# Folding the dimension sums by accumulating transfers, and splitting step 15 of layer 1, in a recommendation tower's interaction layers

## The chip, the core and the metric

The kernel runs on one core of a Trainium2 chip. The metric is the device time of one execution in microseconds. Three executions of the kernel before gave a median of 1453.37 us (1452.75 to 1454.29).

## What is computed

For 2048 samples, 39 embedding rows of 16 numbers each are gathered from 39 tables. Two interaction layers follow, each over the 16 dimensions separately: layer 0 multiplies all pairs of the 39 fields and maps the 39x39 products to 128 values; layer 1 multiplies the 39 fields with the first 64 of these and maps 39x64 products to 128 values. ReLU results are summed over the 16 dimensions, and a small dense tower ends the work.

```python
z0 = jnp.einsum('bid,bjd->bdij', x0, x0).reshape(B, D, F0 * F0)
cur0 = relu(jnp.einsum('bdk,kl->bld', z0, W0))
next_h, direct0 = jnp.split(cur0, 2, axis=1)
z1 = jnp.einsum('bid,bjd->bdij', x0, next_h).reshape(B, D, F0 * Fk)
cur1 = relu(jnp.einsum('bdk,kl->bld', z1, W1))
return jnp.sum(jnp.concatenate([direct0, cur1], axis=1), axis=-1)
```

## The kernel before

The samples go in 16 tiles of 128, and each tile in two units of 8 dimensions (32 units, columns 8 x 128 = 1024). A unit has 6 or 7 steps of layer 0 and 20 steps of layer 1. In each step VectorE (DVE) makes a product tile z of 128x1024 (`make`, L951), and TensorE (PE) multiplies it with weights into PSUM: psA for layer 0, psB for layer 1. The steps of layer 0 of unit u+1 are strewn between the steps of layer 1 of unit u, after the steps listed in `AFTER`.

A step is whole or split. A whole step is one float32 product (`product`, L545). A split step is three float32r products (`split_product`, L575, L578, L582): ScalarE (ACT) rounds z_split to z_hi (`high`, L818), and DVE makes z_lo = z_split - z_hi (`low`, L960), which `low_before` puts on DVE right behind the make of the next step. Layer 0 splits its steps 1 and 4, layer 1 the steps in `SPLIT1`.

Each engine runs its instructions in the order of the code. ACT's `body(u)` issues the `high` of every split step of that body and then, behind all of them, `relu0(u + 1)`: 13 activations that read psA, namely two for h_pair (L763), eight for h_quad (L771), two for h_half (L796) and one for r0 (L802). The `high` of split step 1 of layer 0 of unit u+2 comes behind these on ACT, early in body u+1. `relu1(u - 1)` (L809) is issued at step 6 of body u.

The sums over the dimensions: `relu0` and `relu1` leave the ReLU results in r0 and r1 (128x2048), and DVE reduces each to 128x128 (`sum0`, L1011, every fourth body; `sum1`, L1016, every second body), both at step 18 of a body. `sum1(k)` stands in body 2k+2, `sum0(q)` in body 4q+3; the last of each stands behind the loop.

GpSimd (POOL) issues one indirect gather for each tile and field (L522), 23 for tile 0, 31 for tile 1 and 39 for each later tile, 600 in all. It waits for `x_turned` before tile t, which PE raises when it transposes the tile before the last. SyncE (SP) issues the loads of x_lay, bases, x_more and x_last.

Of the kernel before, what the change touches and what calls it, by code (L numbers as in the profile page):

```python
# [5 lines left out]
P = 128  # L6
B = 2048
F = 39
D = 16
L = 128  # L10
H = L // 2
TILES = B // P
HALVES = 2
UNITS = TILES * HALVES
DH = D // HALVES
C = DH * P
BANK = 512
# [19 lines left out]
LAYS = 1 + FQ  # L37
SPLIT0 = (1, 4)
HALF1 = 12
SPLIT1 = (2, 3, 7, 8, 9, 13, 14)  # L40
WHOLE0 = tuple(s for s in range(STEPS0) if s not in SPLIT0)
REST0 = 3
EARLY = (2, 3)
WHOLE1 = tuple(s for s in range(STEPS1) if s not in SPLIT1 or s in EARLY)
ORDER0 = SPLIT0 + WHOLE0
AFTER = (0, 1, 3, 5, 7, 9, 11)
AHEAD = 2
FIRST_AFTER = (-1, -1, 0, 1, 3, 5, 7)
NZ = 7
NS = 3  # L50
NX = 6
M1, M2 = 512, 256
# [16 lines left out]
ALU = mybir.AluOpType  # L69
ACT = mybir.ActivationFunctionType  # L70
AX = mybir.AxisListType
# [39 lines left out]
def gathers(t):  # L111

    return F - (HOT_F * HOT_GROUPS[t] if t < HOT_TILES else 0)
# [8 lines left out]
def lay_part(s):  # L122

    return divmod(s - (s > HALF1) + 1, 2) if s else (0, 0)


def hot_no(t, q):
# [9 lines left out]
def at1(u, s):  # L137

    return FIRST1[u] + s + sum(a < s for a in after(u))
# [15 lines left out]
def split1(u):  # L155

    return tuple(s for s in SPLIT1 if u > 0 or s not in EARLY)

# [17 lines left out]
def tower(nc, ids, tables, hot_ids, hot_tables, hot_consts, ident_in, dense_t, w0_a, w0_b, w1_whole, w1_split, top, top_small, y):  # L176
    ctx = ExitStack()
    with ctx:
        def sb(name, shape, dt=FP):
            return ctx.enter_context(nc.sbuf_tensor(name, shape, dt))  # L180
# [3 lines left out]
        def sb_loop(name, shape):  # L184
            return loop.enter_context(nc.sbuf_tensor(name, shape, FP))

        def sem(name):
            return ctx.enter_context(nc.semaphore(name))
# [16 lines left out]
        h_half = sb("h_half", [P, BANK])  # L205
        z_hi = [sb(f"z_hi{n}", [P, C], FR) for n in range(NS)]
        z_lo = [sb(f"z_lo{n}", [P, C], FR) for n in range(NS)]
        r0 = sb("r0", [P, 2 * C])
        r1 = sb("r1", [P, 2 * C])
# [3 lines left out]
        w1 = sb("w1", [P, len(WHOLE1), L])  # L213
        w1_hi = sb("w1_hi", [P, len(SPLIT1), L], FR)
        w1_lo = sb("w1_lo", [P, len(SPLIT1), L], FR)
        small = sb("small", [P, K1 + K2 + K2])
        feat_d = sb("feat_d", [P, B // 2])
        feat_side = sb("feat_side", [P, B], FR)
        feat_c = sb("feat_c", [P, B])
# [5 lines left out]
        h_quad = [[sb_loop(f"h_quad{n}_{k}", [P, C]) for k in range(2)] for n in range(2)]  # L225
        z = [sb_loop(f"z{n}", [P, C]) for n in range(NZ)]
        z_split = [sb_loop(f"z_split{n}", [P, C]) for n in range(NS)]
        loop.close()
# [10 lines left out]
        def half(t, u):  # L239
            return t[:, (u % 2) * C:(u % 2 + 1) * C]  # L240
# [18 lines left out]
        more_spread = [t.rearrange("p (d r) -> p d r", d=DH) for t in (feat_c[:, 0:C], feat_c[:, C:2 * C], feat_d[:, 0:C])]  # L259
        left_spread = [r1[:, c * C:c * C + DH * GROUP].rearrange("p (d r) -> p d r", d=DH) for c in range(2)]  # L260

        r0_by_b, r1_by_b = [t[:, :].rearrange("p (b d) -> p b d", d=D) for t in (r0, r1)]

        def lay(u, m):
            n = (LAYS * u + m) % NX
# [3 lines left out]
        w0_raw_b = r0[:, C:C + STEPS0 * L].rearrange("p (s l) -> p s l", s=STEPS0)  # L269
        w1_raw = r1[:, 0:len(SPLIT1) * L].rearrange("p (s l) -> p s l", s=len(SPLIT1))  # L270

# [13 lines left out]
        psB = ctx.enter_context(nc.psum_tensor("psB", [P, 2 * C], FP))  # L285
# [55 lines left out]
        z_lo_made = sem("z_lo_made")  # L341
        relu0_done = sem("relu0_done")
        relu1_done = sem("relu1_done")
        sum0_done = sem("sum0_done")
        sum1_done = sem("sum1_done")
        top_hi_made = sem("top_hi_made")
# [163 lines left out]

        @block.gpsimd
        def _(pool):
            pool.wait_ge(ids_loaded, 16)
            for t in range(TILES):
                if t >= 2:
                    pool.wait_ge(x_turned, t - 1)
                if t == 2:
                    pool.wait_ge(part_spread, 7)
                if t == 1:
                    pool.wait_ge(ids_rest_loaded, 16)  # L520
                for f in range(F - gathers(t), F):
                    nc.gpsimd.indirect_dma_start(emb[t % 2][:, f * D:(f + 1) * D], None, tables[f],  # L522
                                                 bass.IndirectOffsetOnAxis(ids_all[:, t, f:f + 1], 0)).then_inc(gathered[t % 2], 16)


        @block.tensor
        def _(pe):
# [12 lines left out]
            def product(ps, place, k, w, first, last):  # L540

                pe.wait_ge(z_made, place + 1)
                for c in range(C // BANK):
                    cs = slice(c * BANK, (c + 1) * BANK)
                    mm = nc.tensor.matmul(ps[:, cs], w[0:k, :], z[WHOLE_NO[place] % NZ][0:k, cs], start=first, stop=last)  # L545
                mm.then_inc(z_used, 1)

            def half_product(ps, place, w, last):

                pe.wait_ge(z_made, place + 1)  # L550
                for n in range(2):
                    rows = slice(n * HROWS, (n + 1) * HROWS)
                    mm = nc.tensor.matmul(ps[:, n * BANK:(n + 1) * BANK], w[rows, :],  # L553
                                          z[WHOLE_NO[place] % NZ][rows, 0:BANK], start=False, stop=last)
                mm.then_inc(z_used, 1)

            def left_product(u):
# [5 lines left out]
                for k, (v, c) in enumerate(left_groups(u)):  # L563
                    rows = slice(k * GROUP, k * GROUP + LEFT)
                    mm = nc.tensor.matmul(half(psA, v)[:, c * BANK:(c + 1) * BANK], w0[rows, ORDER0.index(STEPS0 - 1), :],  # L565
                                          z[WHOLE_NO[place] % NZ][rows, 0:BANK], start=v > u, stop=v == u)
                mm.then_inc(z_used, 1)

            def split_product(ps, place, k, w_hi, w_lo, first, last):

                n = SPLIT_NO[place]
                pe.wait_ge(z_hi_made, n + 1)
                for c in range(C // BANK):
                    cs = slice(c * BANK, (c + 1) * BANK)
                    nc.tensor.matmul(ps[:, cs], w_hi[0:k, :], z_hi[n % NS][0:k, cs], start=first, stop=False)  # L575
                for c in range(C // BANK):
                    cs = slice(c * BANK, (c + 1) * BANK)
                    nc.tensor.matmul(ps[:, cs], w_lo[0:k, :], z_hi[n % NS][0:k, cs], start=False, stop=False)  # L578
                pe.wait_ge(z_lo_made, n + 1)
                for c in range(C // BANK):  # L580
                    cs = slice(c * BANK, (c + 1) * BANK)
                    mm = nc.tensor.matmul(ps[:, cs], w_hi[0:k, :], z_lo[n % NS][0:k, cs], start=False, stop=last)  # L582
                mm.then_inc(z_used, 1)
# [14 lines left out]
            def step1(u, s):  # L598
# [4 lines left out]
                elif s in split1(u):  # L603
                    n = SPLIT1.index(s)
                    split_product(half(psB, u), at1(u, s), P, w1_hi[:, n, :], w1_lo[:, n, :], s == 0, s == STEPS1 - 1)
# [136 lines left out]
        def _(act):  # L742
# [48 lines left out]
            def relu0_rest(u):  # L791
                h = half(psA, u)
                if u >= 1:
                    act.wait_ge(z_made, at1(u - 1, HALF1) + 1)
                for n in range(2):
                    op = nc.scalar.activation(h_half[n * H:(n + 1) * H, :], h[0:H, n * BANK:(n + 1) * BANK], ACT.Relu)  # L796
                op.then_inc(h_half_made, 1)
                if u >= 4:
                    act.wait_ge(sum0_done, u // 4)
                rows = slice(0, H) if u % 4 >= 2 else slice(H, P)  # L800
                by_d = h.rearrange("p (d b) -> p b d", b=P)[H:P]
                nc.scalar.activation(r0_by_b[rows, :, u % 2 * DH:(u % 2 + 1) * DH], by_d, ACT.Relu).then_inc(relu0_done, 1)  # L802

            def relu1(u):
                act.wait_ge(z_used, at1(u, STEPS1 - 1) + 1)
                if u >= 2:
                    act.wait_ge(sum1_done, u // 2)
                by_d = half(psB, u).rearrange("p (d b) -> p b d", b=P)
                nc.scalar.activation(r1_by_b[:, :, u % 2 * DH:(u % 2 + 1) * DH], by_d, ACT.Relu).then_inc(relu1_done, 1)  # L809

            def high(place):

# [103 lines left out]

            feat_high(0)
            relu1(UNITS - 1)
            feat_high(1)
            top1_keep(0)  # L920
# [17 lines left out]
        def _(dve):  # L938
            def make(place, a, b):
# [6 lines left out]
                else:  # L946
                    n = WHOLE_NO[place]
                    if n >= NZ:
                        dve.wait_ge(z_used, WHOLE_AT[n - NZ] + 1)
                    out = z[n % NZ]  # L950
# [56 lines left out]
                    low(place - 1)  # L1007

            def sum0(q):
                dve.wait_ge(relu0_done, 4 * q + 4)  # L1010
                nc.vector.tensor_reduce(feat_d[:, q * P:(q + 1) * P], r0_by_b, AX.X, ALU.add).then_inc(sum0_done, 1)  # L1011

            def sum1(t):
                dve.wait_ge(relu1_done, 2 * t + 2)
                col = t % 2 * (B // 2) + t // 2 * P
                nc.vector.tensor_reduce(feat_c[:, col:col + P], r1_by_b, AX.X, ALU.add).then_inc(sum1_done, 1)  # L1016

            def split_top():
                dve.wait_ge(top_loaded, 32)
# [196 lines left out]
            feat_low(0)  # L1216
            split_top2()
            sum0(UNITS // 4 - 1)
            sum1(TILES - 1)
            feat_low(1)  # L1220
            hid1_low(0)
# [97 lines left out]
```

## Time and profile before

| | |
|---|---|
| median of 3 runs | 1453.37 us |
| the profiled execution's own time | 1453.96 us |
| its span, first to last instruction | 1452.2 us |
| mean granted TensorE clock | 0.991 of full speed |
| PE busy | 1417.0 us (98%) |
| DVE busy | 1381.2 us (95%) |
| POOL busy | 991.2 us (68%) |
| ACT busy | 784.1 us (54%) |

Busy shares are means over a prologue, 32 unit bodies and a tail. A busy PE is a PE with a product in flight, not one at its peak. A timeline gives starts from the begin of the span; where instructions overlap a little, the distance of two starts is what one of them costs its engine.

### The profile page before, as it was taken

What the parts mean: (1) busy time and instruction counts of PE and PEld (TensorE: products, weight loads), DVE (VectorE), ACT (ScalarE), POOL (GpSimd) and SP (SyncE); (2) the same over time, 40 slices, a digit from 0 to 9 for tenths busy, and PEclk for the clock granted to TensorE, in tenths of its full rate; (3) what the DMA queues carried; (4) which work ended last, traced back from release to release, by engine and by line L of the source; (5) the groups of instructions that cost most, each with busy time, mean ns of one, the idle gap of its engine ahead of it and who ended that gap; (6) DMA issues with size and microseconds to landing.
All of it is one profiled execution on the core that took longest, in us unless ns stands there. A gap on an engine that the chain in (4) does not pass through costs nothing.

```text
span 1452.2 us, 14669 instructions
## 1 busy us (share of the span) xinstructions
PE 1417.0 (98%) x4408; PEld 784.4 (54%) x4408; DVE 1381.2 (95%) x1243; ACT 784.1 (54%) x833; POOL 991.2 (68%) x604
## 2 busy tenths in 40 slices
PE   4899999999999999999999999999999999999999
PEld 3454555555555555555555555555555555555556
DVE  6699999999999999999999999999999999999983
ACT  1454565555455656545465555545556554565655
POOL 7788888888888888888888888888888830000000
PEclk7899999999999999999999999999999999999999
DMA  5879989998888988888898998889898887788600
GB/s 156 177 188 220 223 195 215 203 216 211 201 213 196 214 210 209 212 197 221 199 204 214 210 214 201 208 201 216 200 220 200 203 222 192 204 198 209 178 16 0
DMA packets 130779, 282.64 MB, mean 195 GB/s; under 512 B 36532, under 2 KB 61764, under 8 KB 130572
## 3 DMA queue, kind: packets, MB, share of 16 engines
q1 hardware_dynamic: 96588, 268.31, 75.3%
q0 software_dynamic: 19200, 4.95, 4.0%
q10 hardware_dynamic: 14912, 8.46, 2.0%
q8 instruction: 34, 0.56, 0.2%
q14 instruction: 45, 0.37, 0.1%
HBM read 273.67 MB, written 7.87 MB: 194 GB/s over the span
## 4 chain that ended last, share of the span: by engine, by line
PE 88%; DVE 6%; issue 2%; DMA 2%; POOL 1%; ACT 0%; SPq 0%; DVEq 0%
PE psB L545 42%; PE psA L545 14%; PE psB L575 7%; PE psB L582 6%; PE psB L578 6%; PE psB L553 2%; DVE z L951 2%; PE psA L575 2%; PE psA L578 2%; PE psA L582 2%; POOL emb L522 1%; DVE z_lo L960 1%; DVE z_split L951 1%; PE psA L565 1%; DMA bases<-x_tiles 1%
## 5 line engine op out<-in xcount | busy, mean ns | idle before, releaser
L522 POOL DMA_INDIRECT emb<-in_tbl,ids_all x600 | 991.0, 1652 | 185.0 <-issue 182.6
L545 PE MATMUL psB<-z,w 128*128 128x512 f32 x1544 | 689.1, 592 | 2.1 <-DVE z L951 2.1
L818 ACT ACTIVATE z_hi<-z_split 128x1024 fp32r<-128x1024 f32 x285 | 301.2, 1060 | 508.7 <-DVE z_split L951 446.9
L545 PEld LDWEIGHTS psB<-z,w 128*128 128x128 f32 x1544 | 292.8, 190 | 358.3 <-issue 333.6
L951 DVE TENSOR_TENSOR z<-h_quad,x_lay 128x1024 f32<-128x1024 f32 x354 | 419.4, 1215 | 0.2
L960 DVE TENSOR_TENSOR z_lo<-z_split,z_hi 128x1024 fp32r<-128x1024 f32 x285 | 349.4, 1226 | 14.4 <-ACT z_hi L818 14.4
L951 DVE TENSOR_TENSOR z_split<-h_quad,x_lay 128x1024 f32<-128x1024 f32 x222 | 266.8, 1214 | 3.0 <-DMA x_lay<-x_tiles 3.0
L771 ACT ACTIVATE h_quad<-psA 32x1024 f32<-32x1024 f32 x248 | 251.8, 1015 | 6.6 <-DVE feat_side L1036 2.9
L545 PE MATMUL psA<-z,w 128*128 128x512 f32 x516 | 243.9, 596 | 5.6 <-DVE z L951 5.6
L575 PE MATMUL psB<-z_hi,w_hi 128*128 128x512 f32 x444 | 155.9, 432 | 0.0
L545 PEld LDWEIGHTS psA<-z,w 128*128 128x128 f32 x516 | 98.1, 191 | 105.5 <-issue 92.9
L582 PE MATMUL psB<-z_lo,w_hi 128*128 128x512 f32 x444 | 138.1, 392 | 3.5 <-DVE z_lo L960 3.5
L578 PE MATMUL psB<-z_hi,w_lo 128*128 128x512 f32 x444 | 137.9, 392 | 0.0
L951 DVE TENSOR_TENSOR z<-bases,x_more 128x1024 f32<-128x1024 f32 x96 | 116.6, 1214 | 0.0
L575 PEld LDWEIGHTS psB<-z_hi,w_hi 128*128 128x128 f32 x444 | 79.8, 188 | 52.1 <-issue 38.8
L582 PEld LDWEIGHTS psB<-z_lo,w_hi 128*128 128x128 f32 x444 | 82.4, 188 | 24.8 <-DVE z_lo L960 7.2
L578 PEld LDWEIGHTS psB<-z_hi,w_lo 128*128 128x128 f32 x444 | 83.3, 188 | 18.5
L763 ACT ACTIVATE h_pair<-psA 64x1024 f32<-64x1024 f32 x62 | 62.9, 1014 | 5.7 <-PE psA L565 5.3
L809 ACT ACTIVATE r<-psB 128x1024 f32<-128x1024 f32 x32 | 33.0, 1033 | 45.0 <-PE psB L582 25.2
L575 PE MATMUL psA<-z_hi,w_hi 128*128 128x512 f32 x126 | 52.3, 496 | 0.0
L951 DVE TENSOR_TENSOR z<-bases,x_ring 128x1024 f32<-128x1024 f32 x33 | 40.1, 1214 | 10.2 <-DMA bases<-x_tiles 10.2
L951 DVE TENSOR_TENSOR z_split<-bases,x_ring 128x1024 f32<-128x1024 f32 x31 | 37.7, 1217 | 1.8 <-ACT bases L852 1.1
(122 smaller groups left out, 757.0 us busy)
## 6 DMA issues: line engine op xcount, KB each, us to landing
x_lay<-x_tiles SPq DMA_DIRECT2D x1152, 128.0 KB
x_more<-x_tiles SPq DMA_DIRECT2D x62, 468.0 KB
bases<-x_tiles SPq DMA_DIRECT2D x62, 468.0 KB
x_lay<-x_tiles SPq DMA_DIRECT2D x64, 256.0 KB
x_ring<-x_tiles SPq DMA_DIRECT2D x31, 468.0 KB
emb<-in_tbl,ids_all POOLq DMA_INDIRECT x600
x_last<-x_tiles SPq DMA_DIRECT2D x64, 128.0 KB, 10.3
x_tiles<-x_side ACTq DMA_DIRECT2D x14, 256.0 KB
```

The costliest lines, as they stand in the source:

```text
L522: nc.gpsimd.indirect_dma_start(emb[t % 2][:, f * D:(f + 1) * D], None, tables[f], bass.IndirectOffsetOnAxis(ids_all[:, t, f:f + 1], 0)).th ...
L545: mm = nc.tensor.matmul(ps[:, cs], w[0:k, :], z[WHOLE_NO[place] % NZ][0:k, cs], start=first, stop=last)
L553: mm = nc.tensor.matmul(ps[:, n * BANK:(n + 1) * BANK], w[rows, :], z[WHOLE_NO[place] % NZ][rows, 0:BANK], start=False, stop=last)
L575: nc.tensor.matmul(ps[:, cs], w_hi[0:k, :], z_hi[n % NS][0:k, cs], start=first, stop=False)
L578: nc.tensor.matmul(ps[:, cs], w_lo[0:k, :], z_hi[n % NS][0:k, cs], start=False, stop=False)
L582: mm = nc.tensor.matmul(ps[:, cs], w_hi[0:k, :], z_lo[n % NS][0:k, cs], start=False, stop=last)
L763: op = nc.scalar.activation(h_pair[n * H:(n + 1) * H, :], h[0:H, :], ACT.Relu)
L771: op = nc.scalar.activation(h_quad[u % 2][k][n * QUAD:(n + 1) * QUAD, :], h[k * QUAD:(k + 1) * QUAD, :], ACT.Relu)
L809: nc.scalar.activation(r1_by_b[:, :, u % 2 * DH:(u % 2 + 1) * DH], by_d, ACT.Relu).then_inc(relu1_done, 1)
L818: nc.scalar.activation(z_hi[n % NS][0:k, 0:cols], z_split[n % NS][0:k, 0:cols], ACT.Copy).then_inc(z_hi_made, 1)
L951: nc.vector.tensor_tensor(out[0:k, 0:cols], a[0:k, 0:cols], b[0:k, 0:cols], ALU.mult).then_inc(z_made, 1)
L960: nc.vector.tensor_tensor(z_lo[n % NS][0:k, 0:cols], z_split[n % NS][0:k, 0:cols], z_hi[n % NS][0:k, 0:cols].bitcast(FP), ALU.subtract).th ...
```

## The change

The ReLU results are written in another order (two blocks of four dimensions inside each half of r0 and r1). For all but the last sums, POOL issues two accumulating transfers inside SBUF: the first adds the second half of r0 or r1 (128x1024) onto the first, the next adds 128x512 onto 128x512. DVE then reduces 128x512 to 128x128 in place of 128x2048, and waits for the second transfer (`folded0`, `folded1`). The last sum of each kind stays one reduction, over two axes.

The transfers stand at written places in POOL's list of gathers: the first of `fold1(k)` ahead of the gather of field f of tile t with (t, f) from `FOLDS1`, else (k+4, 8); the second three gathers later; `fold0(q)` in the same way. Ahead of the first POOL waits for the ReLU results, ahead of the second for the first. The folds of the last tiles stand behind all gathers.

Besides, step 15 of layer 1 joins `SPLIT1`: 32 whole steps become split ones.

```diff
-SPLIT1 = (2, 3, 7, 8, 9, 13, 14)
+SPLIT1 = (2, 3, 7, 8, 9, 13, 14, 15)
+FD = 4
+FOLDS1 = {0: (3, 4), 1: (4, 14), 2: (5, 24), 3: (6, 35)}
+FOLDS0 = {0: (3, 20), 1: (6, 4)}
+FOLD_GAP = 3
+def fold1_place(k):
+    return FOLDS1.get(k, (k + 4, 8))
+def fold0_place(q):
+    return FOLDS0.get(q, (2 * q + 4, 25))
...
+            def fold1(k, part):
+                if part == 0:
+                    pool.wait_ge(relu1_done, 2 * k + 2)
+                    nc.gpsimd.dma_start(r1[:, 0:C], r1[:, C:2 * C], accum_op=ALU.add).then_inc(folded1, 16)
+                else:
+                    pool.wait_ge(folded1, 32 * k + 16)
+                    nc.gpsimd.dma_start(r1[:, 0:BANK], r1[:, BANK:C], accum_op=ALU.add).then_inc(folded1, 16)
...
                 for f in range(F - gathers(t), F):
+                    fold_at(t, f)
                     nc.gpsimd.indirect_dma_start(emb[t % 2][:, f * D:(f + 1) * D], None, tables[f],
...
+            fold1(12, 0)
+            fold1(12, 1)
+            fold0(6, 0)
+            fold0(6, 1)
+            for k in (13, 14):
+                fold1(k, 0)
+                fold1(k, 1)
...
-                nc.scalar.activation(r1_by_b[:, :, u % 2 * DH:(u % 2 + 1) * DH], by_d, ACT.Relu).then_inc(relu1_done, 1)
+                nc.scalar.activation(relu_out(r1, slice(0, P), u), relu_in(half(psB, u), slice(0, P)), ACT.Relu).then_inc(relu1_done, 1)
...
             def sum1(t):
                 dve.wait_ge(relu1_done, 2 * t + 2)
                 col = t % 2 * (B // 2) + t // 2 * P
-                nc.vector.tensor_reduce(feat_c[:, col:col + P], r1_by_b, AX.X, ALU.add).then_inc(sum1_done, 1)
+                out = feat_c[:, col:col + P]
+                if t < TILES - 1:
+                    dve.wait_ge(folded1, 32 * (t + 1))
+                    nc.vector.tensor_reduce(out, folded(r1), AX.X, ALU.add).then_inc(sum1_done, 1)
+                else:
+                    nc.vector.tensor_reduce(out, unfolded(r1), AX.XY, ALU.add).then_inc(sum1_done, 1)
```

## Rows read from the trace of the kernel before

**Rows 1.** The page, part 1: busy time and share of each engine.
```profile
PE 1417.0 (98%) x4408; PEld 784.4 (54%) x4408; DVE 1381.2 (95%) x1243; ACT 784.1 (54%) x833; POOL 991.2 (68%) x604
```
**Rows 2.** By window: length; busy PE, PEld, DVE, ACT, POOL; clock, DMA, GB/s.
```profile
650.00:700.00 50.00, 50.00 (x148) 26.71 (x147) 48.40 (x42) 31.23 (x34) 42.69 (x25) 1.00 0.93 218
```
**Rows 3.** DVE's waits from 150 to 1380 us: total us, times, longest.
```profile
DVE z_lo L960 <- ACT z_hi L818: 12.5, 15, 1.4
```
**Rows 4.** Timeline of PE: start, us, what; split steps, then whole ones.
```profile
707.36 0.62 PE L575 MATMUL psB<-z_hi,w_hi 128*128 128x512 f32 x2
...
708.72 1.88 PE L545 MATMUL psA<-z,w 128*128 128x512 f32 x4
710.44 3.60 PE L545 MATMUL psB<-z,w 128*128 128x512 f32 x8
```
**Rows 5.** Timeline of DVE: step 15, then the next body's first z_lo.
```profile
602.92 1.25 DVE L951 TENSOR_TENSOR z<-h_quad,x_lay 128x1024 f32<-128x1024 f32 x1
...
617.70 1.26 DVE L960 TENSOR_TENSOR z_lo<-z_split,z_hi 128x1024 fp32r<-128x1024 f32 x1
...
645.28 1.21 DVE L951 TENSOR_TENSOR z<-h_quad,x_lay 128x1024 f32<-128x1024 f32 x1
646.42 1.21 DVE L960 TENSOR_TENSOR z_lo<-z_split,z_hi 128x1024 fp32r<-128x1024 f32 x1
...
658.98 1.26 DVE L960 TENSOR_TENSOR z_lo<-z_split,z_hi 128x1024 fp32r<-128x1024 f32 x1 [1.13 <-ACT z_hi L818]
```
**Rows 6.** Timeline of ACT: the block `relu0`, then the next z_hi.
```profile
645.44 2.06 ACT L763 ACTIVATE h_pair<-psA 64x1024 f32<-64x1024 f32 x2 [0.22 <-PE psA L565]
...
656.98 1.02 ACT L802 ACTIVATE r<-psA 64x1024 f32<-64x1024 f32 x1
657.91 1.99 ACT L818 ACTIVATE z_hi<-z_split 128x1024 fp32r<-128x1024 f32 x2
```
**Rows 7.** Timeline of DVE: a sum of layer 1 and the instruction behind it.
```profile
608.63 2.27 DVE L1016 TENSOR_REDUCE feat_c<-r 128x128 f32<-128x2048 f32 x1
610.83 1.21 DVE L951 TENSOR_TENSOR z<-h_quad,x_lay 128x1024 f32<-128x1024 f32 x1
```
**Rows 8.** Groups by line: busy us, mean ns; products of 512 columns.
```profile
L951 DVE TENSOR_TENSOR z<-h_half,x_last 128x512 f32<-128x512 f32 x32 | 21.8, 682 | 0.0
```
**Rows 9.** Timeline of POOL: gathers beside that sum, then beside products.
```profile
608.69 0.95 POOL L522 DMA_INDIRECT emb<-in_tbl,ids_all  x1 [0.30 <-issue]
609.94 0.95 POOL L522 DMA_INDIRECT emb<-in_tbl,ids_all  x1 [0.31 <-issue]
...
621.22 1.97 POOL L522 DMA_INDIRECT emb<-in_tbl,ids_all  x1 [0.30 <-issue]
623.49 1.96 POOL L522 DMA_INDIRECT emb<-in_tbl,ids_all  x1 [0.30 <-issue]
```
**Rows 10.** Gathers (L522) up to a time: length, POOL busy (x gathers).
```profile
0.00:161.60 161.60, 129.48 (x97) 0.92 0.80 189
...
0.00:273.30 273.30, 224.28 (x152) 0.95 0.82 196
...
0.00:441.00 441.00, 366.59 (x235) 0.97 0.85 202
0.00:524.60 524.60, 437.64 (x277) 0.97 0.85 202
```
**Rows 11.** Timeline of ACT: the ReLU that completes tile 0 of layer 1.
```profile
165.15 1.02 ACT L809 ACTIVATE r<-psB 128x1024 f32<-128x1024 f32 x1 [2.22 <-PE psB L582]
```
**Rows 12.** DMA issues: KB each, us from issue to landing.
```profile
bases<-in_hot_rows SPq DMA_DIRECT2D x2, 256.0 KB, 3.4
...
r<-in_w_split SPq DMA_DIRECT2D x1, 448.0 KB, 6.0
```
**Rows 13.** Busy time by window, in the prologue (columns as in rows 2).
```profile
50.00:60.00 10.00, 4.85 (x16) 2.18 (x14) 1.53 (x3) 4.98 (x9) 7.79 (x8) 0.87 0.98 209
60.00:70.00 10.00, 9.20 (x16) 3.55 (x16) 7.90 (x11) 0.93 (x3) 7.87 (x8) 0.79 1.06 228
```

More of the change, by code:

```diff
@@ L260, in tower, with relu_out, relu_in, folded @@
         left_spread = [r1[:, c * C:c * C + DH * GROUP].rearrange("p (d r) -> p d r", d=DH) for c in range(2)]
-        r0_by_b, r1_by_b = [t[:, :].rearrange("p (b d) -> p b d", d=D) for t in (r0, r1)]
+        def relu_out(r, rows, u):
+            return half(r, u)[rows].rearrange("p (e b d) -> p e b d", e=DH // FD, d=FD)
+        def relu_in(ps, rows):
+            return ps.rearrange("p (e d b) -> p e b d", e=DH // FD, d=FD)[rows]
+        def folded(r):
+            return r[:, 0:P * FD].rearrange("p (b d) -> p b d", d=FD)
+        def unfolded(r):
+            return r[:, :].rearrange("p (g b d) -> p b g d", b=P, d=FD)
         def lay(u, m):
@@ L343, in tower @@
         relu1_done = sem("relu1_done")
+        folded0 = sem("folded0")
+        folded1 = sem("folded1")
         sum0_done = sem("sum0_done")
@@ L512, in _, with fold0, fold_at @@
         def _(pool):
+            def fold1(k, part):
[5 more added lines that the diff above has]
+                    nc.gpsimd.dma_start(r1[:, 0:BANK], r1[:, BANK:C], accum_op=ALU.add).then_inc(folded1, 16)
+            def fold0(q, part):
+                if part == 0:
+                    pool.wait_ge(relu0_done, 4 * q + 4)
+                    nc.gpsimd.dma_start(r0[:, 0:C], r0[:, C:2 * C], accum_op=ALU.add).then_inc(folded0, 16)
+                else:
+                    pool.wait_ge(folded0, 32 * q + 16)
+                    nc.gpsimd.dma_start(r0[:, 0:BANK], r0[:, BANK:C], accum_op=ALU.add).then_inc(folded0, 16)
+            def fold_at(t, f):
+                for part in range(2):
+                    for k in range(TILES - 1):
+                        if fold1_place(k) == (t, f - part * FOLD_GAP):
+                            fold1(k, part)
+                    for q in range(UNITS // 4 - 1):
+                        if fold0_place(q) == (t, f - part * FOLD_GAP):
+                            fold0(q, part)
             pool.wait_ge(ids_loaded, 16)
@@ L800, in relu0_rest @@
                 rows = slice(0, H) if u % 4 >= 2 else slice(H, P)
-                by_d = h.rearrange("p (d b) -> p b d", b=P)[H:P]
-                nc.scalar.activation(r0_by_b[rows, :, u % 2 * DH:(u % 2 + 1) * DH], by_d, ACT.Relu).then_inc(relu0_done, 1)
+                nc.scalar.activation(relu_out(r0, rows, u), relu_in(h, slice(H, P)), ACT.Relu).then_inc(relu0_done, 1)
             def relu1(u):
@@ L807, in relu1 @@
                     act.wait_ge(sum1_done, u // 2)
-                by_d = half(psB, u).rearrange("p (d b) -> p b d", b=P)
-                nc.scalar.activation(r1_by_b[:, :, u % 2 * DH:(u % 2 + 1) * DH], by_d, ACT.Relu).then_inc(relu1_done, 1)
+                nc.scalar.activation(relu_out(r1, slice(0, P), u), relu_in(half(psB, u), slice(0, P)), ACT.Relu).then_inc(relu1_done, 1)
             def high(place):
@@ L1009, in sum0 @@
             def sum0(q):
+                out = feat_d[:, q * P:(q + 1) * P]
                 dve.wait_ge(relu0_done, 4 * q + 4)
-                nc.vector.tensor_reduce(feat_d[:, q * P:(q + 1) * P], r0_by_b, AX.X, ALU.add).then_inc(sum0_done, 1)
+                if q < UNITS // 4 - 1:
+                    dve.wait_ge(folded0, 32 * (q + 1))
+                    nc.vector.tensor_reduce(out, folded(r0), AX.X, ALU.add).then_inc(sum0_done, 1)
+                else:
+                    nc.vector.tensor_reduce(out, unfolded(r0), AX.XY, ALU.add).then_inc(sum0_done, 1)
             def sum1(t):
@@ L1015, in sum1 @@
                 col = t % 2 * (B // 2) + t // 2 * P
-                nc.vector.tensor_reduce(feat_c[:, col:col + P], r1_by_b, AX.X, ALU.add).then_inc(sum1_done, 1)
+                out = feat_c[:, col:col + P]
+                if t < TILES - 1:
+                    dve.wait_ge(folded1, 32 * (t + 1))
+                    nc.vector.tensor_reduce(out, folded(r1), AX.X, ALU.add).then_inc(sum1_done, 1)
+                else:
+                    nc.vector.tensor_reduce(out, unfolded(r1), AX.XY, ALU.add).then_inc(sum1_done, 1)
             def split_top():
```

## The prediction

> **What bounds the kernel now.** Read the busy shares first [rows 1]: PE 98%, DVE 95%, both means over prologue, loop and tail. A window inside the loop then says which of the two sets the pace: PE is busy in 50.00 of 50 us, DVE in 48.40 [rows 2], so PE leads and DVE has some 3% to spare at most. The waits say what DVE's spare time is spent on: between 150 and 1380 us it waits almost only for ACT's z_hi, 12.5 us in 15 waits [rows 3]. That row is the important one. It isn't PE that holds DVE back, it is ACT, an engine that is busy 54% of the time. The timelines of DVE and ACT show where. At the end of body 13 ACT runs its block of 13 activations, `relu0`, from 645.44 to 657.91 us, 12.47 us without a pause, and the next z_hi (split step 1 of layer 0) starts only then [rows 6]; DVE's z_lo has waited 1.13 us for it [rows 5]. So there is a loop through ACT beside the two busy engines: DVE makes the last split step of a body, ACT rounds it, runs `relu0`, rounds the next body's first split step, and DVE takes the remainder. It is now just hidden: it costs DVE something only where no sum lies at the end of the body (one body in four), and PE nothing.
>
> **What the change gives PE.** A split step takes 1.36 us of PE (707.36 to 708.72), a whole one 1.72 (708.72 to 710.44) [rows 4]. 32 steps give back 32 x 0.36 = 11.5 us, if PE stays the bound.
>
> **What it costs DVE in work.** Each split step adds a z_lo, 1.14 us (645.28 to 646.42) [rows 5]: 4.56 us in four bodies. Four bodies hold three sums, each 2.20 us now (608.63 to 610.83) [rows 7]. The folded sum reads 512 columns; the nearest row for 512 columns is 21.8/32 = 0.68 us [rows 8], so some 0.6 to 0.7, and a sum gives back about 1.55: 4.65 us. Work alone is level, and 1.6 us of stalls in four bodies would still fit. By busy time alone this change is a gain of up to 11 us.
>
> **What it costs the loop through ACT.** ACT issues the `high` of step 15 ahead of `relu0(u + 1)`, since both stand in one body in that order. So `relu0` can't start until DVE has made step 15, and that is two DVE instructions later than step 14, which ends the row of splits now. From the start of step 15's make to the start of the next body's first z_lo the chain then is: the make 1.21 us [rows 5], z_hi 1.0 (1.99 for two), the block 12.47, the next z_hi 1.0 [rows 6], with some 0.1 of hand-over: 15.8 us. Nothing in this chain gets shorter with the sum, as the sum is not on it. In the trace the same distance is 617.70 - 602.92 = 14.78 us with a sum, and 658.98 - 645.28 = 13.70 without [rows 5]. Three bodies of four have a sum: the loop takes (3 x 1.02 + 2.10) = 5.16 us more in four bodies, less a second small wait in the same cycle of about 0.4 (rows 3: 12.5 us in 15 waits, one of 1.13 in each cycle of four bodies), so 4.7, or 1.17 us a body. DVE's own path would be 14.78 + 1.14 - 1.55 = 14.4, so DVE stands still for 1.4 us in each body with a sum and 2.1 in each without, at z_lo; behind it on DVE is the make of step 3, and PE, which in the trace has at most a few us in hand, runs dry. For bodies 1 to 29 that is 29 x 1.17 = 34 us. The passage into the last body and its own additional z_lo (there DVE has nothing to spare) give about 3 more. **Sum so far: +37 us.** I take none of PE's 11.5 us off: PE is no longer the bound.
>
> **What it costs POOL, and who waits for that.** DVE's sum now waits for POOL's second fold, and POOL keeps to its list. So count gathers. `sum1(4)` starts at 524.6 us; its second fold stands behind 23 + 31 + 6 x 39 + 8 + 3 = 299 gathers, and 277 have been issued by then [rows 10]. For `sum1(1)` (149 needed) 152 are there at 273.3; for `sum1(3)` (248) 235 at 441.0 [rows 10]. POOL is ever later, at 363 us / 180 = 2.02 us a gather from 161.6 to 524.6. Why it is that slow is in its timeline: beside products gathers follow each other by 2.27 us, two of DVE's instructions; beside a reduction by 1.25 [rows 9].
>
> At `sum1(4)`: DVE comes 9.5 bodies x 1.17 = 11 us later, which gives POOL 5 gathers more. Ahead of it are 14 fold transfers (eight of `fold1` 0 to 3, four of `fold0`, its own two). No row shows one; bounds are a gather undisturbed, 1.25, and beside products, 2.27 [rows 9]. I take 1.7, between them, as it is not known whether DVE holds them up: 24 us or 12 gathers. At `fold1(0)` POOL comes at 161.6 us [rows 10] and must wait until 166 for the ReLU [rows 11]: with the delay of that ReLU 5 us, 3 gathers. Missing are 299 - 277 - 5 + 12 + 3 = 32 gathers. While DVE waits it holds nothing up, so they take 1.25 us each: 40 us, spread over `sum1` 1 to 4. The last transfer's landing adds about 4 us (256 KB took 3.4, 448 KB 6.0) [rows 12]. In these four bodies the wait for z_hi falls away, as ACT goes on meanwhile: -4 x 1.5. **POOL: +38 us.** From there on two bodies last 86.2 us, or 42.7 gathers; POOL needs 39 and two to four folds of 0.84 gathers, 40.7 to 42.4, and just keeps up. Ends: 0 if POOL should be on time, and 32 x 2.02 + 4 - 6 = 63 if gathers don't get faster while DVE stands.
>
> Two pages of the Trainium skill bear on this price. In "SBUF — State Buffer", section "Who interferes with whom", a DVE instruction with two SBUF inputs is said to hold up a GpSimd instruction that reads SBUF, not one that only writes it. A fold has no index list to read, so by that rule it would go at 1.25 us, 14 would take 17.5 us, and the sum would be 4 us lower; the rows show only gathers. "DMA: Bandwidth & Descriptors", section "Anatomy of one DMA — SWDGE (gpsimd) path", gives about 2.0 us and the bytes over 436 GB/s, an estimate of 2.6 us for the second fold, 1.4 less than what I take from transfers under load.
>
> **Edits at nothing.** The new order of the ReLU results: the same columns read from PSUM with the same stride, 1.02 us each, on ACT behind the block's critical part; r0's is inside the block, and 0.1 us more there would be 3 us in all. The tail keeps its two unfolded sums. Fold traffic is 0.77 MB for each of 22 sums, 17 MB beside some 283; the DMA engines are at 0.93 in a busy window [rows 2], but bodies get 3% longer. I take 0, and up to 10 us for loads that come late.
>
> **The sum.** 1453.96 (the profiled execution; span 1452.2 and 1.8 around it) + 37 + 38 = 1529. It lay 0.6 us above the median of the runs shown: 1528.
>
> **Rivals.**
> 1. Only ACT's loop costs: POOL comes in time, since gathers get faster beside a DVE that stands still 1.4 us in each body and two cheap folds hide among them. 1453.4 + 37 = 1490. Against it: 22 gathers were missing without any fold, and the loop gives back 5.
> 2. The other side, faster: PE stays the bound and its 11.5 us come home, 1442. It decides at one point, whether `relu0` must wait for step 15's `high`. If the block could start behind step 14 as now, the chain would be 2.3 us shorter than DVE's own path in a body with a sum, and if POOL were then also ahead, nothing would wait. For it: busy times are level. Against: ACT's order in the code, and the 1.13 us wait that the trace has already [rows 5].
> 3. POOL stays the bound to the end, or what comes on top is large: folds of 3 us and more (then two tiles of 78 gathers and 6 folds, 158 + 18 and more, pass the 172 us of four bodies), or PE's clock falls in the four long waits. After an idle stretch in the prologue (PE busy 4.85 of 10 us) the granted clock was 0.79 over the next 10 us, part of it at the lower level [rows 13]; that costs about 2 us each time. 1560 to 1590.
> 4. The change doesn't do what it says (places of the folds never bind, step 15 no faster): within 0.2% of 1453, only if both counts above were wrong.
>
> **How the numbers follow.** Forecast 0.62, rival 1 0.16, rival 3 0.14, rival 2 0.05, rival 4 0.03. The range reaches from below rival 1, 1484, to the end that gathers don't get faster with a little of rival 3, 1566; about 2 in 10 lie outside. A measurement of this kernel tells 0.2% (3 us) from no change. Faster 0.05, same 0.02, slower 0.93.
>
> **What would show it.** DVE's waits: z_lo for z_hi some 40 us in place of 12.5, one in nearly each body; four waits of the first folded sums for the folds, 5 to 15 us each, `sum1(4)` the last. PE: idle time of some 90 us, and 1.36 us for step 15. DVE's folded sums at about 0.65 us. ACT's block still 12.5 us, now behind step 15's z_hi. Wrong I would be if gathers ran at 1.7 us beside products, if `relu0` started ahead of step 15's z_hi, or if the block were shorter.

## The result: 10% slower, and where the time went

The changed kernel takes 1596.4 us (median of 5 runs, 1591.9 to 1611.8) against 1453.5 for the kernel before: a ratio of 1.1008, 95% interval [1.0986, 1.103]. The direction was forecast, the size was not: +143 us where +75 was forecast, above the range's end of 1566. The profiled execution took 1611.8 us, the slowest of the five.

First the page, part 1, of the changed kernel (engine, busy us, share of the span, instructions), the line that answers to [rows 1]; then DVE's and POOL's waits (who, for whom, us in total, times, longest), which answer to [rows 3].

```profile
PE 1447.9 (90%) x4472; PEld 801.8 (50%) x4472; DVE 1383.5 (86%) x1275; ACT 814.4 (51%) x865; POOL 957.7 (59%) x648
```
```profile
DVE feat_c L1081 <- DMA r<-r: 128.2, 11, 18.4
DVE z_lo L1017 <- ACT z_hi L875: 33.0, 24, 2.0
...
DVE feat_d L1071 <- DMA r<-r: 7.1, 2, 6.6
```
```profile
POOL r L542 <- ACT r L866: 139.5, 4, 75.4
POOL emb L574 <- PE psA L596: 87.5, 7, 15.1
POOL r L545 <- DMA r<-r: 62.3, 11, 6.7
```

DVE's work has hardly changed (1383.5 against 1381.2 us), as forecast; it now stands still. 135 us of that is for folds, in 13 waits. In the kernel before, DVE's one wait for a transfer of POOL's was 3.5 us for a gather in the prologue. The waits of `sum1` 1 to 4, read one by one, are 13.8, 12.9, 15.4 and 18.4 us; those of `sum1` 5 to 11 are 8.5 to 11.8 us each, 67.7 together. The first four were forecast (44 us, 60.5 came); the other seven were not.

POOL's own waits say why. 87.5 us are for PE's transposes (L596), in seven waits: POOL is not late because it is slow there, it is early, and held up. 62.3 us are for the first fold's landing, ahead of the second (82.6 with three such waits that the list gives no releaser for). (The 139.5 us behind ReLUs are mostly the folds behind the last gather, off the path.)

One pair of bodies shows the ring of waits, on the timelines of PE, POOL and DVE (start, us, what, [idle before, and what ended it]):

```profile
749.09 0.71 PE L596 MATMUL psA<-ident,emb 128*128 128x128 f32 x5
```
```profile
750.07 1.72 POOL L574 DMA_INDIRECT emb<-in_tbl,ids_all  x1 [15.15 <-PE psA L596]
...
766.67 1.00 POOL L542 DMA_DIRECT2D r<-r  x1
...
777.66 0.98 POOL L545 DMA_DIRECT2D r<-r  x1 [5.71 <-DMA r<-r]
```
```profile
776.72 2.35 DVE L1008 TENSOR_TENSOR z<-h_quad,x_lay 128x1024 f32<-128x1024 f32 x2
788.14 0.69 DVE L1081 TENSOR_REDUCE feat_c<-r 128x128 f32<-128x512 f32 x1 [9.07 <-DMA r<-r]
...
882.25 0.69 DVE L1081 TENSOR_REDUCE feat_c<-r 128x128 f32<-128x512 f32 x1 [9.38 <-DMA r<-r]
```

POOL waits until PE has transposed tile 8, gathers eight fields of tile 10 (16.6 us), issues the first fold, waits for it to land, issues the second at 777.66, and that lands some 10 us later. DVE wanted the sum at 779.07 and got it at 788.14. PE then is late by as much, and so is its next transpose, on which POOL waits again: each pair of bodies repeats the wait, and a pair lasts 94.1 us (`sum1` 6 at 788.14, `sum1` 7 at 882.25), against 86.1 in the run below with earlier folds, where no sum waits. The ReLU that the fold needs had been there since 753.7; the fold's place in the list, eight gathers behind a transpose, was 13 us too late.

PE is idle in these waits, and its granted clock falls. By window (length; busy PE, PEld, DVE, ACT, POOL; clock, DMA share, GB/s), beside [rows 2]; then the end of the wait of `sum1` 6 and the time behind it:

```profile
800.00:850.00 50.00, 50.00 (x163) 28.23 (x162) 48.44 (x45) 24.70 (x27) 32.58 (x21) 1.00 0.91 208
850.00:900.00 50.00, 41.81 (x119) 22.55 (x118) 40.62 (x37) 23.88 (x24) 36.34 (x26) 0.90 0.76 183
```
```profile
785.00:790.00 5.00, 0.00 (x0) 0.00 (x0) 1.86 (x3) 1.87 (x3) 3.78 (x5) 0.72 0.78 186
790.00:795.00 5.00, 4.98 (x7) 2.23 (x8) 5.00 (x5) 0.46 (x1) 4.39 (x3) 0.60 0.89 204
795.00:800.00 5.00, 5.00 (x15) 2.58 (x14) 5.00 (x5) 3.59 (x4) 4.09 (x4) 1.00 0.53 137
```

### The profile page after: what moved, and what is told of

Same layout as the page of the kernel before. It is cut to its first block, busy times and chain, and to the rows that moved or that the text cites. A ratio compares the mean times of both kernels' runs of the same rounds, so it can differ in the third digit from the quotient of the medians.

```text
span 1609.9 us, 14991 instructions
## 1 busy us (share of the span) xinstructions
PE 1447.9 (90%) x4472; PEld 801.8 (50%) x4472; DVE 1383.5 (86%) x1275; ACT 814.4 (51%) x865; POOL 957.7 (59%) x648
## 4 chain that ended last, share of the span: by engine, by line
PE 32%; POOL 27%; DMA 16%; DVE 11%; issue 10%; ACT 4%; SPq 0%; DVEq 0%; ACTq 0%
POOL emb L574 26%; PE psB L604 15%; DMA r<-r 14%; PE psA L604 5%; DVE z L1008 4%; DVE z_split L1008 3%; DVE z_lo L1017 3%; ACT h_quad L830 2%; PE psB L634 2%; PE psB L641 2%; PE psB L637 2%; PE psA L637 1%; PE psA L634 1%; PE psA L641 1%; PE psA L624 1%
## 5 line engine op out<-in xcount | busy, mean ns | idle before, releaser
L574 POOL DMA_INDIRECT emb<-in_tbl,ids_all x600 | 914.6, 1524 | 270.1 <-issue 180.2
L604 PE MATMUL psB<-z,w 128*128 128x512 f32 x1416 | 663.9, 614 | 113.5 <-DVE z L1008 113.5
L875 ACT ACTIVATE z_hi<-z_split 128x1024 fp32r<-128x1024 f32 x317 | 334.3, 1060 | 666.9 <-DVE z_split L1008 621.7
L1017 DVE TENSOR_TENSOR z_lo<-z_split,z_hi 128x1024 fp32r<-128x1024 f32 x317 | 387.3, 1222 | 33.1 <-ACT z_hi L875 33.0
L1008 DVE TENSOR_TENSOR z<-h_quad,x_lay 128x1024 f32<-128x1024 f32 x322 | 383.0, 1215 | 0.1
L1008 DVE TENSOR_TENSOR z_split<-h_quad,x_lay 128x1024 f32<-128x1024 f32 x254 | 306.6, 1218 | 6.0 <-DMA x_lay<-x_tiles 4.4
L641 PE MATMUL psB<-z_lo,w_hi 128*128 128x512 f32 x508 | 162.6, 401 | 16.6 <-DVE z_lo L1017 15.1
L634 PE MATMUL psB<-z_hi,w_hi 128*128 128x512 f32 x508 | 175.4, 426 | 0.5 <-ACT z_hi L875 0.5
L637 PE MATMUL psB<-z_hi,w_lo 128*128 128x512 f32 x508 | 157.7, 391 | 0.0
L1081 DVE TENSOR_REDUCE feat_c<-r 128x128 f32<-128x512 f32 x15 | 10.2, 683 | 128.2 <-DMA r<-r 128.2
L542 POOL DMA_DIRECT2D r<-r x15 | 14.8, 985 | 139.5 <-ACT r L866 139.5
L545 POOL DMA_DIRECT2D r<-r x15 | 14.4, 961 | 82.6 <-DMA r<-r 62.3
```

Source lines behind the costliest of these rows:

```text
L875: nc.scalar.activation(z_hi[n % NS][0:k, 0:cols], z_split[n % NS][0:k, 0:cols], ACT.Copy).then_inc(z_hi_made, 1)
L1008: nc.vector.tensor_tensor(out[0:k, 0:cols], a[0:k, 0:cols], b[0:k, 0:cols], ALU.mult).then_inc(z_made, 1)
L1017: nc.vector.tensor_tensor(z_lo[n % NS][0:k, 0:cols], z_split[n % NS][0:k, 0:cols], z_hi[n % NS][0:k, 0:cols].bitcast(FP), ALU.subtract).th ...
```

## The experiments

Two theories stood after the result. ACT: the loop through ACT's block is the larger part. POOL: the folds are. Within POOL, TIE (the ring above) against LANDING AND PACE (too long wherever the folds stand). Each ratio is to the kernel before, measured in the same session (its medians there lie between 1453.0 and 1454.3 us).

**Folds alone.**
```diff
-SPLIT1 = (2, 3, 7, 8, 9, 13, 14, 15)
+SPLIT1 = (2, 3, 7, 8, 9, 13, 14)
```


> The change without the split of step 15: folds, cheap sums and their places as in the change, 7 split steps in layer 1. Theory POOL (folds that land after DVE wants them cost most): waits of the folded sums as in the changed kernel, 135 us or some 10 more, as bodies are 1.2 us shorter and POOL is later by as much; DVE's waits for z_hi back to 15 us or less; 1570 to 1600 us. Theory ACT (the split step and ACT's block cost most, folds little): 1450 to 1470 us.

1579.5 us, 1.0844 [1.0814, 1.0874]. DVE waits 135.3 us in 11 waits for layer 1's folds, as theory POOL said; ACT's theory had 1470 at most. One part missed: the waits for z_hi are 21.9 us, not 15 or less. DVE is busy for 1347.7 us, 33.5 less than before: 1.5 for each of the 22 folded sums.

**Split alone** (the kernel before with step 15 in `SPLIT1`).

> The kernel before with step 15 split, sums unfolded and nothing on POOL. DVE has 1.14 us more in each body and no cheaper sums: its path from step 15 to the next z_lo is 15.9 us with a sum and 15.8 through ACT's block without. Theory ACT and DVE's work: 5.5 us in four bodies more, 1490 to 1498 us, DVE without idle time but for z_hi in one body of four. If the split is hidden: 1442 to 1456 us.

1491.2 us, 1.0256 [1.0235, 1.0276]: as expected, in the lower half of the range. Part 1 of its page, beside [rows 1]:
```profile
PE 1427.2 (96%) x4472; PEld 789.9 (53%) x4472; DVE 1416.8 (95%) x1275; ACT 816.0 (55%) x865; POOL 986.0 (66%) x604
```
DVE has 35.6 us more work, and its waits for z_hi are 19.7 us against 14.4: by itself the split costs through DVE's work and not through the loop. The two halves of the change cost 125 and 37 us by themselves, and 143 together, less than the sum: of the 35.6 us of work the cheap sums take 33.5 off again. The waits for z_hi are 33.0 us with both and 21.9 with the folds alone.

**The loop through ACT's block by itself.**
```diff
                 for f in range(F - gathers(t), F):
-                    fold_at(t, f)
...
-                    dve.wait_ge(folded1, 32 * (t + 1))
                     nc.vector.tensor_reduce(out, folded(r1), AX.X, ALU.add).then_inc(sum1_done, 1)
```


> The change without its 44 fold transfers and without DVE's wait for them: the sums read 512 of the 2048 columns, so three quarters of each sum over the dimensions are left out. DVE's work is that of the change and POOL issues gathers alone. This is the loop through ACT's block by itself. Theory ACT loop: 15.8 us from step 15 to the next z_lo in nearly all bodies, DVE's waits for z_hi some 45 us, 1487 to 1494 us. By busy time alone (PE the bound): 1442 to 1447 us.

1489.7 us, 1.0243 [1.0224, 1.0261]: +35.4 us, forecast +37. Its timelines of DVE and ACT, end of a body without a sum, beside [rows 5] and [rows 6]:

```profile
657.84 1.25 DVE L1000 TENSOR_TENSOR z_split<-h_quad,x_lay 128x1024 f32<-128x1024 f32 x1
...
673.60 1.23 DVE L1009 TENSOR_TENSOR z_lo<-z_split,z_hi 128x1024 fp32r<-128x1024 f32 x1 [1.92 <-PE psA L596]
```
```profile
659.12 1.07 ACT L867 ACTIVATE z_hi<-z_split 128x1024 fp32r<-128x1024 f32 x1 [1.32 <-DVE z_split L1000]
660.09 2.04 ACT L814 ACTIVATE h_pair<-psA 64x1024 f32<-64x1024 f32 x2
...
672.52 1.99 ACT L867 ACTIVATE z_hi<-z_split 128x1024 fp32r<-128x1024 f32 x2
```
From step 15's make to the next body's first z_lo: 673.60 - 657.84 = 15.76 us (forecast 15.8). The block starts behind step 15's z_hi and takes 12.43 us. (The wait is put down to PE here; by ACT's rows it is the z_hi at 672.52.) In the whole run:
```profile
DVE z_lo L1009 <- ACT z_hi L867: 44.0, 29, 2.0
...
DVE z_lo L1009 <- PE psA L596: 5.8, 3, 2.0
```
Together that is 49.8 us against 14.4, 35.4 more: the whole of the loss.

POOL has nothing but gathers here, and yet it waits for PE's transposes, 28.5 us in four waits (17.9 in three with the split alone). So POOL meets this wait when the bodies get longer, without any fold; with the shortened block of the next run it doesn't.

**The block shortened.** The same without folds, and h_half and r0 moved out of the block.
```diff
                     op.then_inc(h_quad_made[k], 1)
-                relu0_rest(u)
...
-                    if s == REST0 and u == 0:
-                        relu0_rest(0)
+                    if s == (REST0 if u == 0 else REST):   # REST = 2
+                        relu0_rest(u)
```


> The run without folds (sums over 512 of 2048 columns), and the last three activations of ACT's block (h_half twice and r0, 2.2 us) moved behind step 2's z_hi of the next body. Theory ACT loop: 13.6 us through ACT against 14.4 on DVE's own path, the wait for z_hi goes in most bodies, PE is the bound: 1440 to 1452 us. If the block is not what sets the pace without folds: no change from the run without folds.

1446.5 us, 0.9946 [0.9928, 0.9965]; DVE's wait for z_hi is 4.6 us in all, and in 50 us PE is busy for 50:
```profile
650.00:700.00 50.00, 50.00 (x152) 27.44 (x151) 49.48 (x45) 32.41 (x35) 42.38 (x26) 1.00 0.89 219
```
2.2 us off the block were worth 43 us: without folds the loop was the bound. It is the case that rival 2 describes, a chain shorter than DVE's own path; the gain on the kernel before is then 7.8 of PE's 11.5 us, with DVE at 49.48 of 50.

**Folds a tile earlier.**
```diff
-    return FOLDS1.get(k, (k + 4, 8))
+    return k + 3, 7
...
-    return FOLDS0.get(q, (2 * q + 4, 25))
+    return 2 * q + 3, 25
...
```


> The change with its folds about one tile earlier in POOL's list: fold1(k) ahead of field 7 of tile k+3, fold0(q) ahead of field 25 of tile 2q+3. Theory TIE (from sum 5 on POOL is not slow: it waits for PE's transpose, which waits for DVE, which waits for POOL's fold, so each pair of bodies repeats the wait of some 9 us): POOL now reaches a fold ahead of the ReLU and waits for that; the second fold lands about 20 us after the ReLU (10 and 7 us of landing, two issues), and the sum comes 23 us after it: waits of the folded sums together under 30 us, 1490 to 1515 us. Theory LANDING AND PACE (two landings and POOL's pace are too long wherever the folds stand): waits of 5 us and more in each sum remain, 1550 us and more.

1496.4 us, 1.0289 [1.0272, 1.0306]: 100 us of the change's 143 come back by moving the folds in POOL's list. No sum waits for a fold, and POOL no longer waits for PE; it waits for ReLUs instead (149.1 us, 74.4 of them in one wait near the end). What is left of the loss is for the most part the loop through ACT:
```profile
DVE z_lo L1013 <- ACT z_hi L871: 45.4, 30, 2.0
```
Theory TIE holds, LANDING AND PACE falls.

**A third buffer for gathered tiles**, so that POOL's wait for a transpose goes while the folds keep their places.
```diff
-NZ = 7
+NZ = 6
...
-                if t >= 2:
-                    pool.wait_ge(x_turned, t - 1)
+                if t >= 3:
+                    pool.wait_ge(x_turned, t - 2)
...
```


> The change with a third buffer for gathered tiles, so that POOL waits for the transpose three tiles back in place of two (to make room NZ is 6 in place of 7). The folds' places stay. Theory TIE: POOL's waits for PE go (87 us in the changed kernel), the waits of sums 5 to 11 (68 us together in the changed kernel) fall to a few us, those of sums 1 to 4 (61 us) stay: 1525 to 1550 us. Theory LANDING AND PACE: POOL was not held up by the tie, sums 5 to 11 wait as before, 1580 to 1605 us.

1552.0 us, 1.0662 [1.0632, 1.0692]. POOL has no wait for PE any more. DVE's waits for layer 1's folds:
```profile
DVE feat_c L1081 <- DMA r<-r: 59.4, 5, 18.4
```
These are `sum1` 1 to 4 (10.7, 13.3, 15.8, 18.4) and 1.2 us of `sum1` 5; 6 to 14 wait for nothing. It takes 2 us more than the range's end (what six z buffers in place of seven cost by themselves no run shows), but it takes the tie apart by its cause: without the wait for the transpose the repeated waits are gone, with the folds at the same places in the list. POOL now stands ahead of ReLUs:
```profile
POOL r L542 <- ACT r L866: 168.3, 10, 76.2
```
So its pace alone would have kept up. The landings didn't stay as they were: issued at another moment, layer 1's folds land in 6.5 and 6.7 us in the median, not 10.7 and 9.8.

**Later sums, folds at the change's places.**
```diff
-                    if s == STEPS1 - 2 and u % 2 == 0 and u >= 2:
+                    if s == SUM1_AT and u % 2 and u >= 3:   # SUM1_AT = 4
                         sum1(u // 2 - 1)
```


> The change with the sum of layer 1 moved from step 18 of an even body to step 4 of the odd body behind it, folds at the change's places. Theory PACE: sums 1 to 4 wait because POOL falls behind by some 15 us in each pair of bodies; 13 us more cover the first of them alone, 40 to 50 us of 61 stay; sums 5 to 11, late by 9 us each through the tie, find their folds landed: 1530 to 1545 us. Theory LANDING: the two landings are what is late in sums 1 to 4, each of them gains 13 us, waits under 15 us together: 1495 to 1510 us. If the tie keeps the lateness at 9 us wherever the sum stands: 1580 us and more.

1563.9 us, 1.0755 [1.0735, 1.0776]; neither range held it. `sum1` 5 to 14 wait for nothing here, which the third case of the expectation, 1580 us, had denied; POOL still waits for transposes (19.1 us in four waits), but the later sum leaves room for that. The early lateness has moved on:
```profile
DVE feat_d L1072 <- DMA r<-r: 35.3, 4, 13.4
...
DVE feat_c L1082 <- DMA r<-r: 25.1, 3, 12.2
```
60 us again (8.9 of them at a later `sum0`), now for the most part at the sums of layer 0, whose folds stand in the same list. So the early lateness belongs to POOL's list as a whole and not to one sum's distance from its ReLU. How much of it is gathers and how much POOL's standing still for a landing isn't settled by this.

**Both causes mended.** The early folds of above with the shortened block; then the sum moved as well.
```diff
-                relu0_rest(u)
...
-                    if s == REST0 and u == 0:
-                        relu0_rest(0)
+                    if s == (REST0 if u == 0 else REST):   # REST = 2
+                        relu0_rest(u)
```
```diff
-                    if s == STEPS1 - 2 and u % 2 == 0 and u >= 2:
+                    if s == SUM1_AT and u % 2 and u >= 3:   # SUM1_AT = 4
```

> Early folds, and the last three activations of ACT's block behind step 2's z_hi of the next body (as in the run that was at 1446 us without folds). If both causes are named rightly they add: bodies of 41.5 us, ReLU to sum 23 us as before, folds just in time or a few us late: 1446 to 1470 us.

> The same, and the sum of layer 1 moved from step 18 of an even body to step 4 of the odd body behind it, some 13 us later, so that the second fold has 36 us from the ReLU on. If the folds' landing is all that is left: no waits for folds, 1443 to 1452 us, faster than the kernel before. If POOL's own load is too high (39 gathers and three transfers a pair of bodies at 2 us): waits grow toward the end, 1455 us and more.

1467.6 us, 1.0109 [1.0068, 1.0151], and 1472.4 us, 1.0118 [1.0093, 1.0143]. The first lies at the upper end of its range: the shortened block is worth 29 us here, where it was worth 43 without folds. The second missed: its waits for folds are gone, but it did not get under 1452, and it is no faster than the first. No wait for a fold is left in either, and 2 to 3 us of waits for z_hi; the largest wait is now for a load:
```profile
DVE z_split L1004 <- DMA x_lay<-x_tiles: 22.1, 13, 3.5
```
(early folds and the shortened block). The same row is 3.6 us in the run without folds and with the shortened block. Between 650 and 750 us (columns as in the windows above) the DMA engines are at 0.89 without folds and at 0.98 with them:
```profile
650.00:750.00 100.00, 100.00 (x314) 55.87 (x313) 99.48 (x90) 59.04 (x63) 85.07 (x50) 1.00 0.89 213
```
```profile
650.00:750.00 100.00, 100.00 (x314) 55.86 (x314) 96.01 (x87) 62.11 (x65) 84.18 (x53) 1.00 0.98 220
```

**Less fold traffic, other orders of loads.**
```diff
-                if q < UNITS // 4 - 1:
-                    dve.wait_ge(folded0, 32 * (q + 1))
-                    nc.vector.tensor_reduce(out, folded(r0), AX.X, ALU.add).then_inc(sum0_done, 1)
...
```
```diff
                     load_base(u + 2, 1)
+                    load_lay(u + 1, 2)
                     load_more(u + 2, 2)
                     load_last(u + 1)
-                    load_lay(u + 1, 2)
```
The first is run by itself (sums of layer 0 unfolded) and the second by itself, both on the version at 1467.6 us, then both together.

> The run at 1467 us with the sums of layer 0 unfolded: 14 of 44 transfers fewer (a third of the fold traffic), DVE 7 x 1.55 = 11 us more, or 1.5 us in four bodies, about what DVE has to spare. Theory LOADS: waits for x_lay fall by a third or more, and the work on DVE takes back about as much: 1455 to 1468 us. If the fold traffic doesn't matter: 1468 to 1478 us.

> Early folds and the rest of ACT's block later (the run at 1467 us), and on SP the load of x_lay for step 3 of the next body ahead of x_more's third part and x_last. In the run at 1467 us DVE waits 22 us for that x_lay and no longer for folds or z_hi. Theory LOADS (the folds' traffic makes loads late, and that is what is left): these waits go, 1444 to 1453 us. If DVE's or POOL's own load is what is left, or the waits only go to another load: 1460 us and more.

> The run with the sums of layer 0 unfolded and the load of x_lay earlier. Theory LOADS: waits for x_lay gone, DVE's work 1.5 us in four bodies above the reordered run with all folds, so DVE and PE about level: 1446 to 1458 us.

A third less fold traffic: 1458.5 us, 1.0043 [1.0028, 1.0058]; 9 us come back although DVE has 10 us more work. The wait for x_lay falls:
```profile
DVE z_split L1001 <- DMA x_lay<-x_tiles: 5.3, 7, 2.9
```
The other order of loads made it no better, rather worse: 1486.1 us, 1.0187 [1.0156, 1.0219], with single runs far apart (1474 to 1495). The waits only go elsewhere, to other loads (`bases`, 26.5 us in 17 waits, and `left_b`, 7.8), the rival case in its expectation, and to z_hi (18.2 in 11). Both together: 1460.2 us, 1.0055 [1.0035, 1.0075], no better than less traffic alone and past its range, though x_lay's waits are gone. So less traffic helped, and this other order did not.

**Does the trade pay at all?** The two side edits (the shortened block and the other order of loads) on the kernel before, as a control; and the version with layer 0 unfolded, with step 15 split in even bodies only.
```diff
-    return tuple(s for s in SPLIT1 if u > 0 or s not in EARLY)
+    return tuple(s for s in SPLIT1 if (u > 0 or s not in EARLY) and (u % 2 == 0 or s != 15))
...
```

> The kernel before with the two side edits alone (rest of ACT's block later, load of x_lay earlier), without folds and without the split of step 15. PE is the bound there already: 1451 to 1455 us, the same. A gain here would say that the gains of the mended versions are not those of the change.

> The run at 1458 us (early folds for layer 1 alone, rest of ACT's block later), with step 15 split in even bodies only: 16 splits in place of 32. In four bodies PE gives back 0.7 us, DVE has 2.3 us more for the splits and 3.1 us less for two folded sums, so PE stays the bound: 1446 to 1452 us if PE's work decides. If DMA waits of DVE remain as large as its small reserve (about 2 us in four bodies): 1453 to 1458 us.

The control is 1453.9 us, 1.0001 [0.9992, 1.001]: the side edits do nothing by themselves. Half the splits: 1452.9 us, 1.0003 [0.9988, 1.0018], between its two cases; waits of 8.5 us for x_lay and 13.5 for z_hi are left. Every repair of the change that computes everything ends at the time of the kernel before or above it; none is faster.

## Why the prediction was right in direction and wrong in size

- **What bounds the kernel: right.** Not PE's 98% but the hidden loop through ACT was the thing to read. Without folds, forecast 1490 (rival 1's time), measured 1489.7; chain forecast 15.8 us, measured 15.76. PE leads by less than [rows 2] suggests, though: that window holds one of the waits for z_hi, and in 200 to 300, 350 to 450 and 550 to 650 us DVE is busy for 50.00 of 50 us as well.
- **PE's share: right.** 1.36 us against 1.72 came home as 7.8 us of 11.5 once the block was shortened (without folds), and not at all in the change.
- **DVE's work: right.** The folded sum takes 0.685 us (forecast 0.6 to 0.7), and DVE's busy time is 2 us above before. The 1.14 us for a z_lo were read off the make ahead of it (645.28); the split alone gives 35.6 / 32 = 1.11.
- **POOL to `sum1(4)`: mechanism right, size off.** 44 us of waits were priced, 60.5 came. The folds' issue was too dear: 0.98 us and 0.30 to the next instruction in place of 1.7. Issues took 0.85 to 1.03 us, beside DVE's products too (the one at 766.67), where gathers take 1.97. With this the rule of the Trainium skill's "SBUF — State Buffer", "Who interferes with whom", agrees: an instruction of GpSimd that only writes SBUF is not held up by a DVE instruction with two inputs there. The landing was too cheap: 4 us priced for the last transfer and none for the first; here 10.7 and 9.8 us in the median for layer 1, and POOL stood still for 4.8 to 9.0 us ahead of the second fold of `sum1` 1 to 11. The rows chosen [rows 12] were loads of the first 17 us. They were not all transfers in a quiet moment: the DMA engines' share was 0.54 in the first 5 us and 1.01 from 10 to 15. Why a fold of 512 KB took 10.7 us, where 448 KB took 6.0 at that share, isn't settled. The estimate from "DMA: Bandwidth & Descriptors" of the Trainium skill, 2.6 us for the second fold, was further off still; the shortest landing of a second fold in this run was 3.4 us.
- **"From there on ... just keeps up": this step failed.** It counted gathers against the time of two bodies and left out POOL's other wait, for the transpose. The count itself was not wrong: with a third buffer POOL arrives ahead of the ReLUs. The kernel before never meets the other wait, so no row shows it; but the wait for `x_turned` is told in the description of the kernel before, and a POOL that is a little faster than longer bodies must run into it, as it does with the split alone and in the run that only lacks the folds. Once DVE waits for POOL, POOL's wait for PE closes a ring, and the fold comes at a fixed distance behind DVE's own progress: 8 gathers, two issues, two landings, 39 us from the transpose at 749.1 to the sum at 788.1, where DVE needs 30 (to 779.1). Nothing in this ring catches up: 67.7 us in `sum1` 5 to 11, forecast 0. Third buffer and earlier folds both take it away. How the 9 us divide between the fold's place and its long landings (20.5 us for the two in the median, 13.2 with the third buffer) isn't settled.
- **The miss, added up.** The profiled execution (1611.8 us) lies 83 above the 1529 forecast for it. 67.7 of that are the ring, 16.5 the step above, 7.1 two sums of layer 0. Off that go some 12, since the loop took less than forecast (waits for z_hi 18.6 us longer than before in place of about 31: a body that waits for a fold has no wait for z_hi). About 4 are left over.
- **Rival 3 named the wrong reasons for its time.** Its 1560 to 1590 was near, but a fold's issue took POOL 1.3 us and not 3, and POOL was not the bound by its pace. The clock did fall (0.90 in the window with a wait; 0.72 in 785 to 790 us, with PE idle, and 0.60 in the next 5, between the levels of 2.4 and 1.2 GHz; 1.00, the upper level, from 795), and it cost next to nothing: a pair of bodies without wait takes 86.1 us, with `sum1` 7's 9.4 of wait and some 1.5 saved at z_hi 94.0, and 94.1 were measured. PE was not the bound there.
- **"Fold traffic: I take 0, up to 10": too low, hidden.** In the change other waits cover it; with these mended the version with folds takes 21 us more than the one without (1467.6 against 1446.5), and the waits for x_lay are 22.1 us against 3.6.

## What to carry to other kernels

An engine that is half idle can still close a loop: look for the wait that is short and regular, follow it to the block of instructions behind which its answer stands, and count what a change puts ahead of that block. When a change makes the bound engine wait for a helper, list everything the helper waits for, also the waits that never bind in the trace of before: if one leads back to the bound engine, the lateness repeats in every round. A transfer that replaces engine work is paid for twice, by its own landing, and by the loads that it makes late.

## What was not expected of the hardware

An accumulating transfer inside SBUF is dear in the DMA engines. DMA queues (packets, MB, share of 16 engines), before and after:

```profile
q0 software_dynamic: 19200, 4.95, 4.0%
```
```profile
q1 hardware_dynamic: 96588, 268.31, 67.3%
q0 software_dynamic: 25536, 22.26, 9.6%
```

The folds' 17.3 MB (the bytes of q0 beyond those of before) took 9.6% of 1609.9 less 4.0% of 1452.2, or 96 us of all 16 engines, 180 GB/s; the plain loads 268.3 MB in 1083 us, 248 GB/s. And their landing depends on where they stand: the first fold of layer 1 (512 KB) took 10.7 us in the median from issue to landing (4.9 to 13.0), that of layer 0, the same size, 6.7; with the folds a tile earlier it was the other way round, 6.4 and 10.2. The DMA share alone doesn't tell it: it was 0.99 while one fold took 10.9 us (from 766.7) and 1.01 while another took 6.4 (from 1321.4, when the gathers were done).
